# The x maxima ahead of the shift, and the shift back behind the h maxima, in the steady rounds of a fused convolution and FP4 feed-forward block

## The reference

```python
xn = _layernorm(x, axis=-1)
x = x + _L0_attn_ref(xn, ...) + _L0_ffn_ref(xn, w_gate, w_up, w_down)
```

```python
scale = jnp.maximum(jnp.max(jnp.abs(xb), axis=-1, keepdims=True) / 6.0, 1e-12)
xn = xb / scale
q = _GRID[jnp.searchsorted(_MID, jnp.abs(xn))] * jnp.sign(xn) * scale

h = jax.nn.silu(fp4_linear(x, w_gate)) * fp4_linear(x, w_up)
return fp4_linear(h, w_down)
```

## Time and profile before

| | |
|---|---|
| median of 3 runs | 137.78 us |
| the profiled execution's own time | 136.63 us |
| span of the profiled execution | 134.8 us |
| busy: VectorE, GpSimd, ScalarE, TensorE matmul | 120.6, 110.4, 98.7, 111.7 us |
| chain that ended last: by engine | POOL 52%, issue 20%, PE 10%, DVE 7%, ACT 6% |
| L1047, L1051, L1077, L1082, L1089 (128 x 704 each) | 885, 894, 899, 891, 886 ns |

### The profile page before, as it was taken

How to read it: one execution, slowest core, us unless ns; L and a number is a source line. 1 busy time by engine, 2 the same in 40 slices (tenths; PEclk the granted TensorE clock), 3 DMA queues, 4 the chain that set the end, 5 groups by cost and what they waited for, 6 DMA issues and landing times.

```text
span 134.8 us, 2143 instructions
## 1 busy us (share of the span) xinstructions
PE 111.7 (83%) x641; PEld 83.7 (62%) x641; DVE 120.6 (89%) x215; ACT 98.7 (73%) x223; POOL 110.4 (82%) x129
## 2 busy tenths in 40 slices
PE   3602789869376999899899999999999999976993
PEld 3501254536243877668786869587868878766882
DVE  0889999999999999979999999999999999899840
ACT  3869966699973899579897889579786648724631
POOL 4568996999699999999999999999999944982220
PEclk9985699986999999999999999999999999999999
DMA  4970000000000000200020020002000200100202
GB/s 125 359 301 9 0 2 0 0 5 0 0 0 0 5 0 0 78 0 0 0 83 0 0 75 12 0 0 78 0 0 0 83 0 0 55 22 5 78 0 80
DMA packets 2891, 4.90 MB, mean 36 GB/s; under 512 B 448, under 2 KB 832, under 8 KB 2880
## 3 DMA queue, kind: packets, MB, share of 16 engines
q1 hardware_dynamic: 2736, 4.77, 9.9%
q10 hardware_dynamic: 144, 0.00, 0.1%
HBM read 2.67 MB, written 2.10 MB: 35 GB/s over the span
## 4 chain that ended last, share of the span: by engine, by line
POOL 52%; issue 20%; PE 10%; DVE 7%; ACT 6%; DMA 2%; POOLq 1%; ACTq 0%
POOL hq L467 9%; POOL y_im L454 6%; POOL y_re L454 6%; POOL xt L411 6%; POOL xt L406 6%; POOL u_im L439 5%; POOL u_re L439 5%; POOL xv L401 3%; DMA par<-params_in 2%; PE ps_g L836 2%; POOL xv L416 2%; DVE bn L975 1%; ACT xbig L633 1%; PE ps_h L871 1%; PE ps_o L892 1%
## 5 line engine op out<-in xcount | busy, mean ns | idle before, releaser
L836 PE MATMUL ps_g<-wg_T,xq_T 128*128 128x352 f32 x64 | 26.6, 498 | 7.2 <-ACT silu L653 4.9
L467 POOL TENSOR_TENSOR hq<-hn,den 128x704 f32<-128x704 bf16 x15 | 20.8, 1387 | 4.3 <-DVE hn L1089 4.3
L892 PE MATMUL ps_o<-wd_T,hq_T 128*128 128x128 f32 x174 | 24.2, 275 | 0.0
L845 PE MATMUL ps_u<-wu_T,xq_T 128*128 128x352 f32 x64 | 22.9, 479 | 0.1
L892 PEld LDWEIGHTS ps_o<-wd_T,hq_T 128*128 128x128 f32 x174 | 22.1, 194 | 0.0
L653 ACT ACTIVATE silu<-ps_g 128x352 f32<-128x352 f32 x32 | 14.7, 461 | 8.4 <-PE ps_g L836 8.2
L659 ACT COPY hq_T<-ps_h 128x384 f32<-128x384 f32 x32 | 15.3, 479 | 5.3 <-PE ps_h L871 5.1
L836 PEld LDWEIGHTS ps_g<-wg_T,xq_T 128*128 128x128 f32 x64 | 10.3, 193 | 13.1 <-ACT silu L653 8.4
L663 ACT ACTIVATE big<-ps_u 128x704 bf16<-128x704 f32 (+1 forms) x17 | 12.2, 725 | 8.2 <-DVE ps_u L1077 8.1
L871 PE MATMUL ps_h<-ident,hq 128*128 128x128 f32 x96 | 16.1, 277 | 2.3 <-ACT hq_T L659 2.1
L871 PEld LDWEIGHTS ps_h<-ident,hq 128*128 128x128 f32 x96 | 11.5, 142 | 9.2 <-ACT hq_T L659 4.2
(11 more groups left out here) (172 smaller groups left out, 258.5 us busy)
## 6 DMA issues: line engine op xcount, KB each, us to landing
x_all<-x_in SPq DMA_DIRECT2D x8, 256.0 KB, 6.5
out<-x_all SPq DMA_DIRECT2D x7, 256.0 KB, 2.0
w_raw<-w_in SPq DMA_DIRECT2D x1, 560.0 KB, 6.2
out<-x_all SPq DMA_DIRECT2D x1, 128.0 KB, 2.1
out<-x_all SPq DMA_DIRECT2D x2, 64.0 KB, 1.6
par<-params_in ACTq DMA_DIRECT2D x1, 3.5 KB, 3.0
```

The costliest lines, as they stand in the source:

```text
L467: pool.tensor_tensor(hq_blocks(q), hn_blocks(q), pair_scales(den[q % 4]), ALU.mult).then_inc(s_hq, 1)
L836: pe.matmul(ps_g[:, 0:I], x_cols(t), wg_T[:, :], start=True, stop=True).then_inc(s_gate, 1)
L845: pe.matmul(slot(q)[:, j, 0:I], x_cols(t), wu_T[:, :], start=True, stop=True).then_inc(s_up, 1)
L892: m = pe.matmul(o, hq_T[t % 3][:, c * P:(c + 1) * P], wd_T[:, c, :], start=False, stop=(c == NCH - 1))
```

## The change

In rounds 4 to 15 of VectorE, the maxima of x now stand between the product and the shift, and the maxima of h between the shift and the shift back. The instructions, their operands, their waits and what they signal stay as they are. No other engine's order is touched.

```diff
             for q in range(SETTLED, NP):
                 g = q // 2
                 product(q)
-                shift_h(q - 1, 0, 0, PAIR)
-                shift_back_h(q - 1, 0, 0, PAIR)
-                amax_h(q)
                 if with_x(q):
                     x_amax((q + 5) // 2, maxima(q)[:, X_COLS])
+                shift_h(q - 1, 0, 0, PAIR)
+                amax_h(q)
+                shift_back_h(q - 1, 0, 0, PAIR)
                 if q % 2 == 0:
                     scan_re(g, q)
```

## The result

The changed kernel takes 139.56 us, the median of six runs (138.40 to 140.46); six runs of the kernel before gave 138.0 (136.59 to 139.62). The changed kernel is slower, by less than the 2% that counts as clear. The forecast was 139.5 us, 1.25% over the 137.78 that stood before.

A forecast was written before the change was run, and what follows sets the result against it. VectorE's order sets the pace, closed into a two-round ring through TensorE and ScalarE with 0.20 us slack. -0.18 + 0.49 + 0.05 + 0.57 + 0.21 + 0 + 0.69 = +1.83 us on the 137.78 median: 139.6, stated 139.5; range 137.1 to 141.0.

The forecast's parts named there:

- VectorE's own saving: VectorE, product to scan: 0.12 us per round from parting shift and shift back, some 0.22 in rounds 7 and 9.
- The rival that 0.93 stays: VectorE's shift keeps the engine 0.93 us whatever follows, so no gain between the shifts; +2.4, 140.2 us, chance 0.08.
- Rounds 4 and 5: Round 5's reciprocal can't start before ScalarE's `den`, limiting the gain to 0.18 us; round 4's 0.12 is worth nothing.
- The ring over the slot: Even round's shift back, then up, gate, silu, `den`, reciprocal, next product: +0.49, +0.05, +0.57, +0.21 us per two rounds, 6 to 13.
- the sum: All predicted gains and costs added, from round 4 to the end: +1.83 us.
- an up pair of 1.45 us: TensorE, rounds 12 and 13: up matmuls that really waited take 1.45 rather than 1.35, which could add 0.1 us.
- Where VectorE would stand still: Reciprocals of rounds 7 and 11 on VectorE released by `den`, idle some 0.5 us.
- The end: Round 15's tight chain, shift back over GpSimd, TensorE and ScalarE to the last `big`, moves later by 0.69 us.
- VectorE's pace: VectorE's gains stand because up matmul or `den` has 0.7 us of unseen room; -0.5, 137.3 us, chance 0.2.
- The ring without slack: TensorE's waiting delays transposes and ScalarE's copies, eating the slacks of all four double rounds; +3.7, 141.5 us, chance 0.12.
- The basis: Profiled execution at 136.63 us lies 1.15 below the 137.78 median; adding to the median gives 139.6, stated as 139.5.

The follow-up runs named there:

- TensorE's move in even rounds alone: Whole change, plus TensorE's up matmuls of the next pair put behind the first output tile's sums in even rounds from 4; 1.0232 of the kernel before.
- the last run: Whole change with round 15 in its old order, and TensorE's up matmuls behind the first output tile's sums in even and odd rounds; 1.0023 of the kernel before.
- Odd rounds alone: Kernel before with VectorE's new order only in odd rounds below 15, old order in even rounds and round 15; 1.003 of the kernel before.
- the old order in round 15: Whole change in rounds 4 to 14, but in round 15 the maxima stand behind the shift back; 1.0132 of the kernel before.
- the double dose: Whole change with the shift back moved further, behind the scans too; 154.65 us in one run.
- shift to SBUF with the order before: Kernel before in its order, but the shift writes to an SBUF tile the shift back reads, and the up matmul waits for the shift; 1.0508.

## Why the prediction was right, point by point

- *VectorE's own saving* (0.12 per round, 0.22 with the x maxima). Right: 0.80 and 3.78 were measured. The rival that 0.93 stays is refuted. The rule of the Trainium skill, VectorE: DVE Perf Modes, section "The DRAIN you can't avoid", that a semaphore costs nothing extra between two operations (measured there on copies), doesn't hold for a shift whose reader follows in these traces: 0.93, where it is 0.80 behind the same shift when an instruction follows that doesn't read it.
- *Rounds 4 and 5* (-0.18): -0.16, with the reciprocal of round 5 waiting 0.45 us for `den`.
- *The ring over the slot* (+0.49, +0.05, +0.57, +0.21): +0.50, +0.03, +0.57, +0.31. In rounds 6 and 7 the cause is shown: with TensorE's move in even rounds alone the 0.50 is gone, with VectorE's order as in the change. That the hand-over of the slot is behind the loss of all four is shown by the last run, which takes it away with VectorE's order of these rounds left as it was. In rounds 10 to 13 it isn't shown that the even round's hand-over is the one that costs: freeing it alone brought nothing there (25.10 against 24.69), and late shift backs in odd rounds alone cost +0.59 and +0.46. That the sum came out at +0.57 there is in part luck: two rings of nearly the same length meet, and only one had been counted.
- *The 0.1 too little in rounds 12 and 13.* The text named an up pair of 1.45 us as possible. It wasn't that: the up matmul of round 12 takes 1.35, as before. It starts at 107.07, 0.17 after the shift back ends at 106.90 and not 0.05, as TensorE comes late by its own order.
- *Where VectorE would stand still.* In round 7 `den` was late by 0.45, as said. In round 11 I expected the same; there the 0.57 went into three waits, 0.37 for the turned state (in round 10, ahead of anything that the shift back of round 10 could delay), 0.24 for `big` and a little for `den`. The reciprocal of round 11 still starts 0.03 after `den`, so the ring that I counted is closed as well. TensorE was idle for the shift back by 0.33, 0.33 and 0.19 us in rounds 6, 8 and 10, where I expected some 0.5: it comes later by itself.
- *The end* (+0.69): +0.71, and taken back by the old order in round 15 (13.51).
- *What was incomplete.* The text held that odd rounds don't matter, as the shift back of an odd round isn't in the ring, and put their effect into the rival without slack. Odd rounds alone cost 0.98 us, where the whole change costs 1.41. The prediction would have been wrong for that half of the change.
- *The rivals.* VectorE's pace (faster) had its gains right and its premise wrong. The ring without slack described the way over the copies and the turned state correctly, and the double dose showed it at full size. With the change that way is open too (the 0.37 us for the turned state in round 10), but its size was wrong: the waits for `den` in rounds 7, 9, 11 and 13 were 0.45, 0.31, none over 0.2 and 0.71, not over 0.8 in all of them.
- *The basis.* The 0.94 us ahead of round 4 belongs to the execution, not to the change: 0.90 of it is there at the first product (at 22.70 instead of 21.80), which waits 0.93 us for its up matmul. Ahead of that, two gate matmuls took 1.51 us instead of 0.83, with the granted clock at 1.00 in both executions; why, I leave open. That the medians hit 139.5 against 139.56 is closer than the sum deserves: 1.5% of the runs before is 2.1 us, the profile from round 4 on says 1.96, the sum said 1.83.

## What to carry to other kernels

When the order on the busiest engine is changed, list for each moved instruction who is released by it, and compare its end with the start of the first one released, to a tenth of a microsecond: a hand-over that shows in no wait can still be tight, because the released engine arrives at the same moment. A saving on the busiest engine is worth only as much as the slack of the ring through the other engines; where two such rings are nearly of one length, count both: freeing one of them brought nothing in four of the eight rounds here. And where a release must come later, look for work on the released engine that can go ahead of it; do so in every round of the pattern, or the loss moves to the other one.

## What the runs showed of the hardware

A scalar_tensor_tensor with one operand in PSUM and one in SBUF takes 886 ns for 128 x 704 in the kernel before. With both in SBUF (shift to SBUF with the order before) it took, from round 5 on, 1.71 to 1.73 us in five rounds and 0.89 to 0.93 in the six others. At 78.13 it starts while a GpSimd instruction runs, from 77.83 to 79.09, and takes 1.72. At 72.22 it starts first and takes 0.92, and the GpSimd multiplication that starts at 72.35 is stretched, from 1.05 (at 48.45 in the same execution) to 1.70 us:

```profile
72.22 0.92 DVE L1090 SCALAR_TENSOR_TENSOR hn<-big,ht 128x704 bf16<-128x704 bf16 x1
...
78.13 1.72 DVE L1090 SCALAR_TENSOR_TENSOR hn<-big,ht 128x704 bf16<-128x704 bf16 x1
```

```profile
72.35 1.70 POOL L402 TENSOR_TENSOR xv<-xn,inv 128x512 f32<-128x512 f32 x1
...
77.83 1.26 POOL L407 TENSOR_TENSOR xt<-xbig,xv 128x512 f32<-128x512 f32 x1
```

The Trainium skill, SBUF — State Buffer, section "Who interferes with whom", says that a VectorE instruction with two SBUF inputs contends with a GpSimd instruction that reads SBUF, and that whoever issues first blocks the other. These rows agree, in both directions. Until the tile was moved this kernel had one of the two operands in PSUM in the product, the division, the shift and the shift back of every whole pair.
